# The last chunk of a DLRM tower: layer 2 of tile 13 into a lookup bank, pair transposes of tile 14 and a last turn issued sooner, two blocks between the gram halves of tile 15, and the last bias added by a matmul

## The reference, cut to what matters

```python
e = jnp.stack([tbl_0[ids[:, 0]], ..., tbl_25[ids[:, 25]]], axis=1)      # 2048 x 26 x 128
combined = jnp.concatenate([e, r_dense_x[:, None, :]], axis=1)          # 27 rows a sample
interact = jnp.einsum('bfd,bgd->bfg', combined, combined)
z = interact[:, _TRIU_I, _TRIU_J]                                       # 351 pairs a sample
h = jnp.concatenate([z, r_dense_x], axis=1)                             # 479
h = jnp.maximum(h @ W_top1 + b_top1, 0.0)                               # 512
h = jnp.maximum(h @ W_top2 + b_top2, 0.0)                               # 256
y = h @ W_top3                                                          # 1
```

## Time and profile before

| | us |
|---|---|
| median of 3 executions | 367.49 |
| lowest and highest | 365.63, 367.98 |
| the profiled execution's own time | 366.74 |
| its span, from first to last instruction | 365.0 |
| TensorE busy | 333.1 (91% of the span) |
| VectorE busy, ScalarE busy | 182.8, 178.4 |
| GpSimd busy | 259.1 |
| mean granted clock of TensorE | 0.991 |

### The profile page before, as it was taken

One profiled execution on the slowest core, in us unless ns is written; L12 is line 12 of the kernel. 1 busy time (PEld: TensorE's weight loads), 2 busy tenths in 40 slices (PEclk: granted clock), 3 DMA queues, 4 the chain that ended last, 5 costly groups with the idle time before them and its releaser, 6 DMA issues.

```text
span 365.0 us, 12417 instructions
## 1 busy us (share of the span) xinstructions
PE 333.1 (91%) x5536; PEld 274.6 (75%) x5536; DVE 182.8 (50%) x436; ACT 178.4 (49%) x234; POOL 259.1 (71%) x265
## 2 busy tenths in 40 slices
PE   1999889698999999999999999999999999969876
PEld 0488767486887888877887878877887898857765
DVE  3699954545255635555356635565345644212112
ACT  2499731563625734383535834284544734364222
POOL 6778777777777777777777777777777777777100
PEclk9999999899999999999999999999999999999899
DMA  7979394243243233334143333334252222222100
GB/s 229 346 212 265 101 291 118 53 113 90 61 125 82 81 95 95 88 80 121 52 126 82 81 96 95 88 76 127 55 126 82 66 54 66 54 58 55 29 4 3
DMA packets 19513, 37.59 MB, mean 103 GB/s; under 512 B 5541, under 2 KB 8229, under 8 KB 19460
## 3 DMA queue, kind: packets, MB, share of 16 engines
q1 hardware_dynamic: 11268, 20.00, 18.9%
q0 software_dynamic: 8192, 16.79, 17.6%
HBM read 36.77 MB, written 0.01 MB: 101 GB/s over the span
## 4 chain that ended last, share of the span: by engine, by line
PE 57%; POOL 21%; issue 10%; DVE 5%; ACT 4%; DMA 3%; SPq 0%; DVEq 0%
PE ps_lk L568 22%; POOL rows L268 21%; PE ps_gram L594 10%; PE ps_mlp L621 5%; PE ps_zt L621 5%; PE ps_tr L579 4%; DVE onehot L303 3%; PE ps_lk L544 3%; PE ps_mlp L628 2%; PE ps_zt L628 2%; PE ps_lk L641 2%; DMA h<-in_tbl 2%; ACT xt L395 1%; DMA rows<-in_tbl,gather_ids 1%; DVE table L309 1%
## 5 line engine op out<-in xcount | busy, mean ns | idle before, releaser
L268 POOL DMA_INDIRECT rows<-in_tbl,gather_ids x256 | 257.7, 1007 | 79.0 <-issue 77.1
L303 DVE TENSOR_SCALAR onehot<-ids 128x512 fp32r<-128x512 f32 (+1 forms) x328 | 125.8, 438 | 73.8 <-PE ps_lk L568 40.6
L568 PE MATMUL ps_lk<-onehot,table 128*128 128x512 f32 (+1 forms) x704 | 154.8, 374 | 5.6 <-DVE onehot L303 3.8
L568 PEld LDWEIGHTS ps_lk<-onehot,table 128*128 128x128 f32 x704 | 120.1, 190 | 27.4 <-issue 4.2
L405 ACT COPY xt<-ps_tr 128x512 f32<-128x512 f32 x64 | 76.8, 1201 | 106.9 <-PE ps_tr L579 106.8
L594 PE MATMUL ps_gram<-xt 128*26 128x26 f32 x4096 | 53.0, 192 | 8.2 <-issue 3.8
L594 PEld LDWEIGHTS ps_gram<-xt 128*26 128x26 f32 x4096 | 44.0, 103 | 21.8 <-issue 18.6
L317 DVE STREAM_TRANSPOSE zs<-ps_gram 128x832 f32<-128x832 f32 x16 | 16.8, 1050 | 78.3 <-PE ps_gram L594 78.3
L392 ACT COPY xt<-ps_lk 128x512 f32<-128x512 f32 x35 | 42.0, 1234 | 21.3 <-issue 9.5
L579 PE MATMUL ps_tr<-ident,rows 128*128 128x128 f32 x256 | 39.5, 276 | 4.3 <-DMA rows<-in_tbl,gather_ids 2.2
L579 PEld LDWEIGHTS ps_tr<-ident,rows 128*128 128x128 f32 x256 | 30.2, 140 | 11.6 <-issue 5.8
(11 more groups left out here) (55 smaller groups left out, 140.4 us busy)
## 6 DMA issues: line engine op xcount, KB each, us to landing
ids<-in_ids_onehot SPq DMA_DIRECT2D x41, 256.0 KB, 3.5
rows<-in_tbl,gather_ids POOLq DMA_INDIRECT x256
w<-in_tbl SPq DMA_DIRECT2D x6, 512.0 KB, 6.8
zt<-in_tbl SPq DMA_DIRECT2D x3, 512.0 KB, 7.0
dense_x<-in_dense SPq DMA_DIRECT2D x8, 128.0 KB
zt<-in_dense SPq DMA_DIRECT2D x8, 128.0 KB, 2.3
h<-in_tbl SPq DMA_DIRECT2D x1, 512.0 KB, 6.1
w<-in_w SPq DMA_DIRECT2D x1, 512.0 KB
```

Source lines behind the costliest of these rows:

```text
L268: pool.indirect_dma_start(rows[n % ROW_BUFS][:, r, :], None, t_[f"tbl_{GATHERED[r]}"], bass.IndirectOffsetOnAxis(ap=gather_ids[:, n, r:r + ...
L303: nc.vector.tensor_scalar(onehot[:, k, 0:w], ids[e % IDS][:, 0:w].bitcast(F32), float(k), None, ALU.is_equal).then_inc(s_unit, 1)
L568: m = nc.tensor.matmul(ps_lk[e % LB][:, x], table[:, i, part, k, :], onehot[:, k, x], start=(k == 0 and j == 0 and part == 0), stop=(k == ...
```

## The change

Five things change, all in or just ahead of the last chunk.

1. Layer 2 of tile 13 goes into `ps_lk[2]` rather than `ps_zt`. `turn_pairs(14)` then waits for the last relu of the chunk before instead of `head(13)`, and is issued between the layer 2 of tile 12 and that of tile 13.
2. `turn(15, 3)` is issued after `last1(0, 0)` rather than after `last1(0, 1)`, and ScalarE's copy of it one place earlier too.
3. `last1(0, 3)` is issued ahead of `gram(15, 1)` and no longer behind it.
4. `last1(0, 2)`, which writes `ps_lk[2]`, waits for `head(13)`.
5. For tile 15, the bias is written into the bank by a matmul of the identity with the bias rows (`bias_first`) between `last1(1, 0)` and `last1(1, 1)`; layer 2 accumulates on it, and VectorE's addition goes.

```diff
         def head_bank(n):
             if n >= TILES - CT:
                 return (ps_tr, ps_mlp)[n % CT][:, 0:H2]
+            if n >= TILES - 2 * CT:
+                return (ps_mlp, ps_lk[2])[n % CT][:, 0:H2]
             return mlp_bank(T1 + n % CT)[:, 0:H2]
...
             def head(n):
                 m, t = divmod(n, CT)
+                if n == TILES - 1:
+                    dve.wait_ge(s_head, n)
+                    dve.sem_inc(s_carrier["dve"], 1)
                 dve.wait_ge(s_mlp, last(t) + LAST_USES if m == CHUNKS - 1 else m * MLP_USES + T1 + t + 1)
-                nc.vector.tensor_tensor(head_bank(n), head_bank(n), heads[:, 0, :], ALU.add).then_inc(s_bias, 1)
-                dve.wait_ge(s_bias, n + 1)
+                if n < TILES - 1:
+                    nc.vector.tensor_tensor(head_bank(n), head_bank(n), heads[:, 0, :], ALU.add).then_inc(s_bias, 1)
+                    dve.wait_ge(s_bias, n + 1)
...
             last_relu1(0, 0)
+            evac_group(a + 1, 3)
             last_relu1(0, 1)
-            evac_group(a + 1, 3)
             last_relu1(0, 2)
...
                 if t > 0:
                     pe.wait_ge(s_zt, n)
+                elif m == CHUNKS - 1:
+                    pe.wait_ge(s_act, LAST_ACT)
                 elif m > 0:
                     pe.wait_ge(s_head, m * CT)
...
-                elif t == 0 and j == LB:
+                elif t == 0 and j >= LB - 1:
                     pe.wait_ge(s_head, TILES - CT)
...
-                                         start=(k == 0), stop=(k == T1 - 1))
+                                         start=(k == 0 and t == 0), stop=(k == T1 - 1))
...
+            def bias_first():
+                nc.tensor.matmul(head_bank(TILES - 1), ident[:, :], heads[:, 0, :], start=True, stop=False)
...
             layer2(c - 1, 0)
+            turn_pairs(a)
             layer2(c - 1, 1)
-            turn_pairs(a)
             last1(0, 0)
+            turn(a + 1, 3)
             last1(0, 1)
-            turn(a + 1, 3)
             gram(a + 1, 0)
             last1(0, 2)
+            last1(0, 3)
             gram(a + 1, 1)
-            last1(0, 3)
...
             for j in range(T1):
                 last1(1, j)
+                if j == 0:
+                    pe.wait_ge(s_act, LAST_ACT + T1)
+                    bias_first()
```

## The result

The changed kernel takes 362.96 us (median of 7 executions, 361.76 to 363.91), against 366.49 (7 executions) for the kernel before. The ratio is 0.9886, with a 95% interval of 0.9857 to 0.9916; a second set gave 0.9883 (0.9843 to 0.9923). The ratio stands for 4.2 us less, 3.1 to 5.2 by the interval, where 4.47 were forecast; the two medians are 3.53 us apart.

What follows compares the result with a forecast made beforehand. TensorE, busy 91% of the span, sets the pace but stops five times in the last 28 us. Gains of 4.43 and 0.04 sum to 4.47 us: 362.27 from 366.74, raised half way toward the median to 362.6; range 361.0 to 364.6.

Steps and rivals of the forecast that it cites:

- pairs of tile 14 sooner: Tile 14's pair transposes ahead of layer 2 of tile 13: `last1(0, 0)` starts at 341.37 instead of 343.41, 2.04 us.
- from `last1(0, 0)` to the first gram half (clock, turn): This stretch of TensorE takes 2.99 us instead of 5.42: 2.43 us gained, 1.3 of it the clock.
- gram halves and what is between: Both tile 15 halves and what stands between take 4.91 us instead of 4.84, the second half's pause 0.35: 0.07 us lost.
- VectorE's pack: Packing of tile 15 sets when its pair transposes start: 351.77, 4.43 us sooner, against 4.40 remaining after the halves.
- from the pair transposes to the end (bias): Tile 15's bias as matmul costs TensorE 0.43 us and saves VectorE an instruction of 0.44: net gain 0.04 us.
- Clock: At `last1(0, 0)`: with TensorE busy ahead of it the granted clock does not fall, worth 1.3 us.
- The second rival: The low clock near 343.5 was that execution's: other executions of before at 365.4, gain 3.2 us; chance 0.12.
- Turn sooner: `turn(15, 3)` starts at 342.46, so the first gram half starts at 344.36 after a hole under 0.4 us.
- the first rival: The pause in the second gram half is not the packets' and comes back whole: 0.84 us more, 363.4; chance 0.14.
- Cover: Behind the second gram half, without `last1(0, 3)`, TensorE idles about 1.0 us while VectorE packs tile 15; no loss.

Runs made afterwards that it cites:

- the shifted kernel: The kernel before with 64 transposes of the identity (128 TensorE instructions) put at its start; tail 24.11 us, its one execution 373.76 us.
- the second repeat of the kernel before: The unchanged kernel before, profiled again, second of three more profiles; the tails of the three and the first lie from 25.16 to 25.68 us.
- 16 of the 47 above: Of 47 executions of the kernel before timed beside other kernels, those with mean clock 0.995: 365.8 us on the mean; the other 31 take 367.8.
- The filled kernel: The kernel before with four matmuls of 128 columns in the hole behind layer 2 of tile 13; median 366.87 us, ratio 1.0002; again 366.46, 0.9982.

## Why the prediction was right, and where it was not

| step | forecast | first profiles |
|---|---|---|
| pairs of tile 14 sooner | 2.04 | 2.05 |
| from `last1(0, 0)` to the first gram half (clock, turn) | 2.43 | 2.63 |
| gram halves and what is between | -0.07 | 0.27 |
| VectorE's pack | 0.03 | 0.07 |
| from the pair transposes to the end (bias) | 0.04 | -0.01 |
| sum | 4.47 | 5.01 |

**Pairs sooner** came out to the hundredth, and the head of tile 13 costs nothing: it ends at 343.83, 2.9 us before `last1(0, 2)`.

**Clock.** I had it at 1.3 us and it is 1.6. I priced a block of layer 1 at 1.09 us, from a row with a gram half ahead of it and one behind it (350.01 to 351.10). The changed profile has 0.99 where a gram half is on one side only (346.72 to 347.71, and 347.71 to 348.70) and 0.89 where none is (342.74 to 343.63). The same error made the halves' row too dear by 0.2 us. That the fall comes with the hole is shown by the profiles: it is in four of the five that have both holes, 1.08 and 0.62 us, and in none of the nine that lack the first. The hole is not enough by itself: the shifted kernel has both and kept full clock. The second rival rested on an idler stretch, 320.0 to 323.6 us, behind which the clock stayed full. In six of the other thirteen profiles it did fall right behind that place; in the second repeat of the kernel before it was 0.57 from 324 to 328 us. So the same place can bring a fall in one execution and none in the next.

The rival that the fall was one execution's luck is out as it stood, by four profiles of four. But it put the other executions at 365.4 us, and 16 of the 47 above, likely those without the fall, have a mean of 365.8. The changed kernel's 13 timed executions have one of 363.1: that is 2.7 us under these 16 and 4.7 under the other 31. The filled kernel's times do not show 1.6 us. So this share of the gain is shown in profiles and not in times.

**Turn sooner.** Shown: 0.89 us by undoing it.

**Gram halves.** The mechanism is confirmed: pauses behind matmul 43, 107 and 35 are where counting instructions puts them. The border that I put 70 instructions into the second half is there, behind matmul 35. The size varies: with one block between the halves the hole was 0.82 to 1.45 us in nine profiles, with two blocks 0.3 or less in five. The view counts a hole from the end of the last matmul, some 0.2 us behind its issue. By starts, the second half took 1.40 to 1.66 us in those five, 0.2 to 0.5 over the 1.2 of a half without a pause; I had 0.35 and 1.55, in the middle. I mixed the two accounts in the first rival's price: 1.19 us of idle time before are 2.57 less 1.2, some 1.4 us by starts, so a pause that stayed whole would have cost 1.0 us more and not 0.84. The first rival, that it comes back whole, is out, and so is, for this place, the Trainium skill's rule (Runtime: NRT & Kernel Launch, instruction fetch mechanics) that the fetch is mostly hidden.

**Cover.** The hole is 0.66 us and not 1.0. The view counts it from the end of the last matmul, some 0.2 us after its issue, from which I had counted; and `dense_rows` took 0.77 us behind a gram half (350.10 to 350.87) against 0.67. Neither costs anything.

**Bias.** Even, as forecast.

**The number.** 362.6 us were forecast and 362.96 measured. In the profiles the tail gained 0.54 us more than I had and began 1.38 us later, and 0.33 us of the forecast was a step half way to a median of three. That the number is so close is in part luck; the steps are what was tested.

**What is left.** By the tails, four of before (mean 25.5) and two of the changed kernel (20.8), the gain is 4.7 us; by the times it is 3.1 to 5.2. In the four profiles of before the tail starts at 338.1 us on the mean, in the nine of kernels with another tail at 338.8. TensorE's list is the same up to there (apart from the shifted kernel, left out here). A fall of the clock at 324 to 328 us does not make it, since two of the four have one and three of the nine. Whether that 0.7 us is chance is open.

## What to carry to other kernels

Price a reordering at the end of a kernel from marks inside the stretch that it touches, since the untouched part differs by more than a microsecond between executions. Where an engine takes very short instructions by the hundred, count them: here a packet's worth, 256 instructions, that ran in less than the 3.2 to 3.8 us until the next one could be used was followed by a pause that no semaphore explains, and a block of work moved in between took the pause's place and more. A hole that waits for another engine is the place for work that is due later on the full path: the bias matmul there hid its 0.43 us. And before you call a fall of the clock regular or rare from a few profiles, hold their mean clock against that of all timed executions.

## What the runs showed of the hardware

- A pause of TensorE that is labelled "issue" moved with the count of instructions: 128 put at the program's start, over 5,000 passes of other work ahead, moved it from behind matmul 43 to behind 107, as packets of 256 would have it. It ended 2.4 to 2.8 us after one packet of the instruction queue.
- The same block of eight passes over 128 columns issues in 0.89, 0.99 or 1.09 us, with matmuls of 26 columns on neither side, on one or on both.
- A hole of 1.08 us followed by one of 0.62 brought the half clock in four profiles of before, and not in the shifted kernel; with the first hole filled, in none of two. Sixteen matmuls of layer 1 issue in 3.48 us at the half clock and in 1.78 to 1.89 at the full one.
